# Three attentions of a four-block transformer: projection and core in one program

## The reference, cut to what matters

```python
qkv = x @ w_qkv.T + b_qkv + x @ lora_A.T @ lora_B.T
q, k, v = heads of qkv                       # B * 12 heads, N = 256 tokens, 16 channels
attn = einsum('bqc,bkc->bqk', q * SCALE, k)
Rh, Rw = rel_pos_h[coords], rel_pos_w[coords]        # (16, 16, 16) each
rel_h = einsum('bhwc,hkc->bhwk', r_q, Rh)
rel_w = einsum('bhwc,wkc->bhwk', r_q, Rw)
attn = softmax(attn + rel_h[..., :, None] + rel_w[..., None, :])
out = (attn @ v) @ w_proj.T + b_proj
```

## Time and profile before

| what | before |
|---|---|
| median of 3 runs | 935.94 us |
| profiled execution | 933.57 us, its span 931.9 us |
| PE / DVE / ACT / POOL busy | 695.0 / 407.1 / 302.9 / 100.4 us |
| l0, start of projection to first look | 15.2 to 52.5 us |
| l2, the same | 414.2 to 468.1 us |
| l3, the same | 733.7 to 787.9 us |
| granted clock of the span | 0.845 |

### The profile page before, as it was taken

One profiled execution on the slowest core, in us unless ns is written; L12 is line 12 of the kernel. 1 busy time (PEld: TensorE's weight loads), 2 busy tenths in 40 slices (PEclk: granted clock), 3 DMA queues, 4 the chain that ended last, 5 costly groups with the idle time before them and its releaser, 6 DMA issues. The chain is left out here.

```text
span 931.9 us, 13079 instructions
## 1 busy us (share of the span) xinstructions
PE 695.0 (75%) x4086; PEld 565.0 (61%) x4086; DVE 407.1 (44%) x1030; ACT 302.9 (33%) x650; POOL 100.4 (11%) x117
## 2 busy tenths in 40 slices
PE   5659975898988999339379980299990692999497
PEld 2346744596774999316367770299980381676477
DVE  3438863315255333154358844033311553676501
ACT  2213433132223544114224441044440250444322
POOL 3021110002000000340100003300006101000000
PEclk9959997598988999759679985599995595899789
DMA  3662201443014453113774204347612058441053
GB/s 108 183 176 77 73 20 35 111 110 109 1 43 110 132 150 108 51 38 110 176 163 121 83 6 129 116 112 178 178 58 78 0 153 214 114 123 50 15 132 109
DMA packets 85888, 94.42 MB, mean 101 GB/s; under 512 B 16797, under 2 KB 73393, under 8 KB 85829
## 3 DMA queue, kind: packets, MB, share of 16 engines
q1 hardware_dynamic: 80948, 82.27, 32.5%
q0 software_dynamic: 4368, 11.21, 4.5%
q10 hardware_dynamic: 528, 0.39, 0.1%
HBM read 68.18 MB, written 25.89 MB: 101 GB/s over the span
## 5 line engine op out<-in xcount | busy, mean ns | idle before, releaser
L838 DVE TENSOR_REDUCE neg_max<-psum 128x4 f32<-128x1024 f32 x72 | 88.0, 1222 | 78.8 <-PE psum L736 77.3
L805 ACT ACTIVATE area<-psum 128x512 f32<-128x512 f32 x144 | 79.0, 599 | 97.1 <-PE psum L749 97.1
L736 PE MATMUL psum<-k_parts,q_parts 128*128 128x256 f32 x288 | 57.1, 324 | 60.2 <-DMA k_parts<-k_scratch 56.2
L1617 PE MATMUL psum<-w,area 128*112 128x192 f32 (+1 forms) x576 | 96.2, 326 | 0.0
L1617 PEld LDWEIGHTS psum<-w,area 128*112 128x112 f32 (+1 forms) x576 | 93.4, 183 | 0.0
L736 PEld LDWEIGHTS psum<-k_parts,q_parts 128*128 128x128 f32 x288 | 42.3, 206 | 76.8 <-DMA k_parts<-k_scratch 57.8
L356 PE MATMUL psum<-ident,x_norm 128*96 128x128 f32 x128 | 25.4, 340 | 76.2 <-DVE x_norm L329 53.4
L785 PE MATMUL psum<-area,v_stage 128*32 128x256 f32 x576 | 79.2, 392 | 3.5 <-ACT mix_chan L811 3.4
L748 PE MATMUL psum<-q_parts,k_parts 128*128 128x256 f32 x288 | 77.7, 300 | 1.0 <-DVE shift L848 1.0
L749 PE MATMUL psum<-shift,ones_r 128*128 128x256 f32 x288 | 75.5, 292 | 0.0
L1707 DVE TENSOR_TENSOR q_parts<-w,q_parts 128x1536 fp32r<-128x1536 f32 x16 | 28.1, 1758 | 89.8 <-ACT q_parts L1641 89.8
(11 more groups left out here) (215 smaller groups left out, 1179.7 us busy)
## 6 DMA issues: line engine op xcount, KB each, us to landing
w<-in_f_w_dram SPq DMA_DIRECT2D x32, 576.0 KB, 4.6
q_parts<-q_scratch SPq DMA_DIRECT2D x204, 64.0 KB, 2.3
k_parts<-k_scratch SPq DMA_DIRECT2D x108, 64.0 KB, 2.4
w<-in_f_w_dram SPq DMA_DIRECT2D x16, 384.0 KB, 4.5
w<-in_f_w_dram SPq DMA_DIRECT2D x32, 192.0 KB, 5.2
q_scratch<-k_parts SPq DMA_DIRECT2D x6, 384.0 KB, 4.0
q_scratch<-w SPq DMA_DIRECT2D x6, 384.0 KB, 4.6
sorted_scratch<-zeros POOLq DMA_DIRECT2D x1, 2304.0 KB, 10.2
```

The source lines that it names most:

```text
L736: ins = pe.matmul(ps[:, b, IMG_TOK * c:IMG_TOK * (c + 1)], query(2 * s + b, c), k_parts[:, 2 * s + b, :], start=True, stop=True)
L805: act.activation(net.probs_t[:, s % 2, b, :, :].rearrange("p k t -> p (k t)"), ps[:, 2 + 2 * (s % 2) + b, :], ACT.Exp).then_inc(exp_done, 1)
L838: ins = dve.tensor_reduce(most, ps[:, 0:2, :].rearrange("p b (c k) -> p (b c) k", c=2), AX_X, ALU.max, negate=True)
L1617: ins = pe.matmul(ps[0:R, 6 + c // 2, D * (c % 2):D * (c % 2 + 1)], x.hidden[:, fc, R * c:R * (c + 1)], net.w2[:, b, fc, :], start=(fc == ...
```

## The change

Both blocks become one, `attention`, so no engine waits for all others between projection and core. Within it:

- TensorE's order becomes queries, table products, keys, values. A table product takes both halves at once: 32 products of 128 columns instead of 64 of 64. rel_w's table copies go to ScalarE, rel_h's stay on VectorE, 6 each.
- The units are ordered queries, rel_h, rel_w, keys. Of each unit image 0 is written first (96 KB a part) and loaded as soon as it is written: SyncE waits for the write's semaphore, then issues the load. The rest is written later: queries' images 1 to 3 at once, after that of all other units image 1, then images 2 and 3.
- A load covers 6 heads (96 KB) instead of 4 (64 KB): 20 loads an image instead of 30 in l2 and l3, 12 instead of 18 in l0. Image i+1's half is loaded once image i's 6 heads are scored.
- `prep.third` in l0 is issued after all writes, ahead of image 1's loads.
- GpSimd loads the constant rows in 2 DMAs instead of 6, while the projection runs.
- The parts lie in other places of the same tiles; x_norm serves as room for one.

```diff
-def attention_project(net, m, prep=None):
-def attention_core(net, m):
+def attention(net, m, prep=None):
+    units = [(kind, half) for kind in (*range(kinds), KEY) for half in range(2)]
...
+    def project_tensor(pe):
...
+        for b in range(4):
+            channels(0, b // 2, b % 2, b)
+        if not m.local:
+            pe.wait_ge(q_sb, 4)
+            pe.wait_ge(table_act, 1)
+            pe.wait_ge(table_dve, 1)
+            for kind in range(2):
+                for b in range(4):
+                    for n in range(REL):
+                        pos = REL * b + n
+                        q = query[:, :, pos, :] if kind == 0 else query[:, :, :, pos]
+                        ins = pe.matmul(ps[0:HC, 4 * (1 - kind) + b, P * n:P * (n + 1)], net.rel[:, kind, pos, :], q,
+                                        start=True, stop=True)
+                    ins.then_inc(rel_ps, 1)
+        for b in range(4):
+            if not m.local:
+                pe.wait_ge(rel_h_sb, b + 1)
+            channels(1, b // 2, b % 2, 4 + b)
...
+    def project_scalar(act):
...
+        take_high(act, 0, 2)
+        if not m.local:
+            for b in range(4):
+                act.wait_ge(rel_ps, b + 1)
+                act.copy(rel_h[:, :, REL * b:REL * (b + 1), :],
+                         ps[0:HC, 4 + b, :].rearrange("p (a n b) -> p n a b", a=REL, b=SIDE)).then_inc(rel_h_sb, 1)
+            act.wait_ge(rel_h_sb, 4)
+            act.wait_ge(rel_ps, 8)
+            take_high(act, 2, 4)
+            act.wait_ge(low_sb, 2)
+            act.wait_ge(rel_w_sb, 4)
+            take_high(act, 4, 6)
+        for half in range(2):
+            act.wait_ge(k_sb, 2 * half + 2)
+            take_high(act, 2 * kinds + half, 2 * kinds + half + 1)
...
+    def project_vector(dve):
...
+        take_low(dve, 0, 2)
+        if not m.local:
+            for b in range(4):
+                dve.wait_ge(rel_ps, 4 + b + 1)
+                dve.tensor_copy(...).then_inc(rel_w_sb, 1)
+            take_low(dve, 2, 4)
+        keys(0)
+        take_low(dve, 4, 2 * kinds)
+        take_low(dve, 2 * kinds, 2 * kinds + 1)
+        keys(1)
+        values(0)
+        take_low(dve, 2 * kinds + 1, 2 * kinds + 2)
+        values(2)
...
         @block.sync
         def _(sp):
...
+            def load_unit(sp, n):
+                sp.wait_ge(first_written[n], 2 * DMA)
+                for part in range(2):
+                    load(sp, 0, units[n][1], units[n][0], part)
+            def load_image(sp, i):
+                for half in range(2):
+                    sp.wait_ge(scored, i * HEADS + (HALF_HEADS * (half + 1) - HEADS))
+                    for kind in (*range(kinds), KEY):
+                        for part in range(2):
+                            load(sp, i, half, kind, part)
+            for n, (kind, half) in enumerate(units):
+                for part, ready in ((0, high_sb), (1, low_sb)):
+                    sp.wait_ge(ready, n + 1)
+                    store(sp, kind, half, part, 0, 1, first_written[n])
+                if kind == 0 and half == 1:
+                    load_unit(sp, 0)
+                    load_unit(sp, 1)
+                    for rest in range(2):
+                        for part in range(2):
+                            store(sp, 0, rest, part, 1, IMGS, rest_written[0])
+                elif 0 < kind < KEY and half == 1:
+                    load_unit(sp, n - 1)
+                    load_unit(sp, n)
+                elif kind == KEY:
+                    load_unit(sp, n)
+            for n, (first, last) in enumerate(((1, 2), (2, IMGS))):
+                for kind, half in units[2:]:
+                    for part in range(2):
+                        store(sp, kind, half, part, first, last, rest_written[n])
+            if prep:
+                start_loads(net, sp, prep.third, prep.loaded)
+            sp.wait_ge(rest_written[0], DMA * (4 + 2 * (len(units) - 2)))
+            load_image(sp, 1)
+            sp.wait_ge(rest_written[1], DMA * 2 * (len(units) - 2))
+            with sp.Fori(2, IMGS) as i:
+                load_image(sp, i)
...
             def look(i, s):
-                if s % 2 == 0:
-                    pe.wait_ge(loaded[s // 2], i * per_load + per_load)
-                    pe.wait_ge(const_loaded[s // 2], DMA * (3 if m.local else 2))
+                if s % (PAIRS // 2) == 0:
+                    pe.wait_ge(loaded[s // (PAIRS // 2)], i * per_load + per_load)
```

More of the change, by code:

```diff
@@ L658, in attention_core, with scratch @@
     K0 = 64
+    REL = 4
+    units = [(kind, half) for kind in (*range(kinds), KEY) for half in range(2)]
+    first_written = [sem(f"{tag}_first_written{n}") for n in range(len(units))]
+    rest_written = [sem(f"{tag}_rest_written{n}") for n in range(2)]
+    query, rel_h, rel_w = (v.rearrange("p h t -> p (h t)").rearrange("p (n a b) -> p n a b", a=SIDE, b=SIDE)
+                           for v in (parts.query, *parts.rel_values))
+    def scratch(kind, half, part):
+        rows = slice(HC * half, HC * (half + 1))
+        return net.k_dram[part, rows] if kind == KEY else net.q_dram[part, kind, rows]
@@ new lines, in store, with load @@
+    def store(eng, kind, half, part, first, last, done):
+        src = (parts.high, parts.low)[part][kind][half]
+        src = src.bitcast(F32) if part == 0 else src
+        eng.dma_start(scratch(kind, half, part)[:, first:last, :],
+                      src.rearrange("p (i t) -> p i t", i=IMGS)[:, first:last, :]).then_inc(done, DMA)
+    def load(eng, i, half, kind, part):
+        if kind == KEY:
+            dst, places = k_parts, (QROWS,) if part else (0, K0)
+        else:
+            dst, places = q_parts, (K0 * part + HD * kind,) + ((QROWS,) if (part, kind) == (0, 0) else ())
+        src = scratch(kind, half, part)[:, i, :].rearrange("(n c) t -> c n t", n=HALF_HEADS)
+        for at in places:
+            eng.dma_start(dst[at:at + HD, HALF_HEADS * half:HALF_HEADS * (half + 1), :].bitcast(F32), src).then_inc(loaded[half], DMA)
@@ L660, in group @@
     def group(g):
         return slice(GH * g, GH * (g + 1))
-    heads = "(n c) t -> c n t"
-    def rows_of(g):
-        return slice(HD * GH * g, HD * GH * (g + 1))
-    def load_q(eng, i, g):
-        places = [(K0 * part + HD * kind, part, kind) for part in range(2) for kind in range(kinds)] + [(QROWS, 0, 0)]
-        for at, part, kind in places:
-            eng.dma_start(q_parts[at:at + HD, group(g), :].bitcast(F32),
-                          net.q_dram[part, kind, rows_of(g), i, :].rearrange(heads, n=GH)).then_inc(loaded[g], DMA)
```

324 lines of the change are left out of this document (120 added, 204 removed).

## The result

The changed kernel takes **956.82 us** (median of 4 runs, 952.50 to 961.19) against 935.28 for the kernel before (4 runs): 1.023 times as long, 95% interval 1.018 to 1.029. The forecast was 917.2, range 908 to 929. The forecast had the direction wrong, and the figure is close to that of the rival "six-head loads become the bound in the loop" (954).

What follows compares the result with a forecast made beforehand. The prediction took TensorE's waits for loads, 56.2 us in 6 waits, as the bound; l0 +1.7, l2 -10.1 and l3 -10.3 gave -18.7, so 914.9 from the profiled 933.57, or 917.2 as a median, range 908 to 929.

Steps and rivals of the forecast that it cites:

- six-head loads become the bound in the loop: Loop over images: at 0.89 us a load each half is late by 4.1 us, 954 in all; chance 0.07.
- First look of l2 at 455.9: Start of l2's core: first look at 455.9 instead of 468.1, 12.2 us earlier.
- The 24 writes: l2, ahead of image 1's loads: SyncE begins 24 writes at 457.8 and ends at 468.6.
- Image 1's loads: l2, behind the writes: 10 loads, last issued at 473.0, landed at 475.4, so image 1 begins 12.4 us earlier.
- Late by 0.45 us. Five halves in images 1 to 3: 2.3 us a core: Loop of l2 and l3: a half is ready at 8.6 us, needed at 8.15; five such waits cost 2.3 us.
- the 914.9 of the sum: Whole kernel: the profiled execution's 933.57 less 18.7 from l0, l2 and l3.
- 0.70 us an issue if it goes by bytes: Loop's 96 KB loads: the bound not taken; 64 KB's own figures were taken as the nearer.
- the turn of sign: Loop's six-head loads: from 0.68 us a load on, the change was said to lose time instead of gaining.
- l0 +1.7: l0: first look's 9.5 us gain given back, half clock adds 1.8; +1.7 in all, between -1 and +7.
- Rivals on the writes and on the 30 loads: Writes ahead of image 1 take 21 us: 933, chance 0.10; l0's 30 loads take 28 us: 924, chance 0.16.
- holds the first three: Claim that range 908 to 929 covers forecast, kinder and 30-loads cases, plus the faster part of the writes case.
- the kinder case: Table products in l2 and l3: clock stays up or rel_w is weight-bound, 911.6; both, 905; chance 0.20.

Runs made afterwards that it cites:

- m1_loads: The network left out, only loads in stretches of ten, of 3 to 12 heads, on one or two queues; no time to compare.
- b_six: The kernel before with one part of the change alone, images 1 to 3 loaded by six heads: 976.83 us, ratio to before 1.044 to 1.050.
- a_grp: The changed kernel with images 1 to 3 loaded by four heads again, image 0 still by six: 923.24 us, ratio to before 0.987 to 0.992.

## Why the prediction was wrong, step by step

- **First look of l2 at 455.9**, from a start at 414.2: 41.7 us. Measured 42.1. Right, with its parts: the second key bank was taken at 449.43, 29.1 us into the stage (28.8 predicted); the table products took 10.69 us (10.2), with rel_w's instructions at 182 ns before the clock fell (22 in the 4 us from 437 to 441) and not 208; the clock fell in rel_w (0.59 from 441.0 to 443.4, where rel_w ends, then 0.50 to 447.6). l3's first look came 10.7 us earlier, 1.2 less than l2's; the prediction had them alike.
- **The 24 writes**: 463.95 to 476.6, 12.6 us; I had 10.8. 1.8 us off.
- **Image 1's loads**: from 476.6 to look at 486.69, 10.1 us; I had 6.8. Together image 1 is 5.1 us later than the 475.4 of the prediction. This is the failed term's first place: 0.98 MB into 16 partitions a load at 105 GB/s need 9.4 us, an estimate from m1_loads.
- **"Late by 0.45 us. Five halves in images 1 to 3: 2.3 us a core"**: the step that failed. Ready 1.86 + 4.25 + 2.4 = 8.5 was wrong at the landing: 1.86 + 9.2 = 11.1, needed at 8.15, late by 2.9. Measured in b_six's l2: 2.78 to 3.19. In the changed kernel the loop lost 17.8 us in l2 from image 1's look to the end (the expectation of b_six has 17.9): 10.0 in waits and 7.8 in slower steps, for which l2's and l3's sums had no term. Of the 7.8 some 2.2 stand behind image 1's own wait, for a_grp, without any wait in its loop, has them too (49.2 us from image 1's look to the end, 47.1 before; granted clock 0.50 from 484.43 to 488.0). Some 5.6 are left for the loop's waits; in b_six's l2 it is 5.3 (23.1 less 17.8).
- **The difference as a whole.** 961.19 less the 914.9 of the sum is 46.3 us. Image 1 is 5.2 and 4.7 us later than forecast in l2 and l3, the two loops lost 17.8 and 17.5 instead of 2.3 each, l0 is 4.4 over: 45.0 together.
- **How it failed.** The bound was in the text: "0.70 us an issue if it goes by bytes", and so was the turn of sign, from 0.68 on. The bound lay beyond the turn, and yet the range stopped at 929. I took the near end because a 96 KB write lands in 2.1 us. But that write leaves 96 partitions and the load enters 16; the nearest row by bytes wasn't the nearest by shape. The fit of 2.0 us + bytes / 436e3, which the prediction quotes from the Trainium skill, DMA: Bandwidth & Descriptors, section Anatomy of one DMA, stands there for DMAs from GpSimd's queue and has no term for the partitions: by it 96 KB land 0.08 us after 64 KB, measured are 0.5 for a load alone (2.6 and 2.1) and 1.1 in stretches of ten (3.5 and 2.4). And DMA shares of 0.4 to 0.5 under 64 KB loads read as room: in m1_loads the share is 0.37 at 102 GB/s, 0.60 at 104 and 0.97 at 105. Ten four-head loads stood where issue (6.45 us) and rate (0.66 MB at 105 GB/s, 6.2 us) meet.
- **The rival at 954** had the place, the sign and nearly the time, with a wrong inner cause: it let the issue grow to 0.89 us, and the issue stayed at 0.47. That its time came so near is luck: its lateness of 4.1 us a half was 1.1 to 3.0, and the clock, the later image 1 and l0 made up the difference.
- **l0 +1.7**: measured +6.1. The 30 loads took 21.4 us (20.9 predicted), from 50.4 (48.9); image 1's look came at 79.44 instead of 75.4, 4.6 us behind its last issue and not 2.4. The narrow load accounts for part: 0.59 MB at 105 GB/s are 5.6 us from 71.82, so 77.4; the other 2 us are open. The prediction also had this look before at 75.5, from its maximum; the trace has 74.85. So l0 lost 4.6 us there and 1.5 behind it, where the sum had nothing and 1.8. Its range, -1 to +7, held.
- **Rivals on the writes and on the 30 loads**: neither decided; the writes took 12.6 us where the rival had 21, the 30 loads 21.4 where it had 28.

One slip in the text had no part in it: the range "holds the first three", but the kinder case's 905 lies below its 908.

Open: why one strip of 16 partitions, ten times over, is slower (11.52 us) than eight in turn (9.16), and 48 x 4 slower than 32 x 6; and why two queues into the two halves of SBUF gain 20%. Why the clock falls behind some waits and not behind others is open too. A layout in DRAM that would let a load fill 48 partitions at once wasn't tried.

## What to carry to other kernels

A DMA's price has three parts: its issue, its landing, and the rate at which its own partitions take data. Making loads fewer and larger saves the first and, if they enter few partitions, leaves the last, so a prefetch with 8 us of slack can't hold more than that rate gives. Look for the row that is nearest in shape, not in bytes. And where the bound that you write down lies beyond the point where the sign turns, the range has to hold what it gives.

## What the runs showed of the hardware

- A load's issue on SyncE took 0.45 us at 48, 64, 96 and 192 KB alike in m1_loads (0.47 in the networks); its size shows in the landing (medians of a stretch's seven query loads 2.1, 2.4, 3.5 and 7.6 us). Behind 24 writes in the changed kernel's l2 seven issues took 4.65 us, 0.66 each.
- Ten loads into 16 partitions each came to 102 to 107 GB/s over a stretch, 85 if all entered the same 16. A second queue made 108 of it in the same strips, 128 if it entered the other 64 partitions. 1.97 MB took 18.75 us into 16 partitions a load, 12.83 into 48, 10.93 into 32, 9.96 into 96.
- The DMA share of a window is not the share of a limit: it went from 0.37 to 0.97 at 102 to 105 GB/s.
- In the changed kernel a wait of 2.80 us was followed by 4.2 us at a granted clock of 0.63, in which the steps are slower. Not every such wait was: behind one of 3.19 us in b_six the clock stayed at 1.00, as this window shows (columns as in the loop windows above).

```profile
488.90:493.00 4.10, 4.01 (x32) 3.29 (x33) 2.44 (x4) 1.09 (x2) 0.00 (x0) 1.00 0.18 56
```
